# A two-layer decoder on one core: transposed copies of x made by VectorE and DMAs instead of TensorE, in cross attention and in local attention

## The reference

```python
x = _layernorm(x + _L0_attn_ref(x, ...))            # state space model
x = _layernorm(x + _L0_xattn_ref(x, ctx, ctx, mask, ...))   # cross attention
x = _layernorm(x + _L0_ffn_ref(x, ...))             # three linears, tanh
x = _layernorm(x + _L1_attn_ref(x, ...))            # local attention
x = _layernorm(x + _L1_xattn_ref(x, ctx, ...))
x = _layernorm(x + _L1_ffn_ref(x, ...))

def _L0_xattn_ref(q, k, v, mask, ...):
    qh = (q @ Wq.T + bq) ...                         # 16 heads of 32
    ...
    scores = jnp.where(mask, einsum('bhqd,bhkd->bhqk', qh, kh) / sqrt(D_K), -1e9)
    out = einsum('bhqk,bhkd->bhqd', softmax(scores), vh) ...
    return out @ Wo.T + bo

def _L0_ffn_ref(x, weight, aux_weight1, aux_weight2, bias):
    ...
    return jnp.tanh(x @ weight @ aux_weight1 @ aux_weight2 + bias)

def _L1_attn_ref(x, Wg, bg, Wv, bv, Wo, bo):
    g = x @ Wg.T + bg
    v = x @ Wv.T + bv
    ...
```

## Time and profile before

| | us |
|---|---|
| median of 3 runs | 2664.42 (2663.80 to 2665.64) |
| the profiled execution's own time | 2665.74 |
| its span in the trace | 2664.0 |
| TensorE busy | 2535.6 (95%) |
| VectorE busy | 1933.4 (73%) |
| GpSimd busy | 867.0 (33%) |
| ScalarE busy | 732.0 (27%) |

### The profile page before, as it was taken

One profiled execution on the slowest core, in us unless ns is written; L12 is line 12 of the kernel. 1 busy time (PEld: TensorE's weight loads), 2 busy tenths in 40 slices (PEclk: granted clock), 3 DMA queues, 4 the chain that ended last, 5 costly groups with the idle time before them and its releaser, 6 DMA issues. The chain is left out here.

```text
span 2664.0 us, 37090 instructions
## 1 busy us (share of the span) xinstructions
PE 2535.6 (95%) x12933; PEld 1562.9 (59%) x12933; DVE 1933.4 (73%) x3292; ACT 732.0 (27%) x1073; POOL 867.0 (33%) x900
## 2 busy tenths in 40 slices
PE   8999998999999898999998869999999999999998
PEld 4444544555555444445444447777777777777775
DVE  4788403666667446777778858888888888888886
ACT  1111222333332125666668711000000000000000
POOL 2322203455555336767677721111111111111000
PEclk9999999999999999999999989999999999999999
DMA  5444121000000043343434441222222222222111
GB/s 177 146 143 178 56 91 42 1 0 1 1 1 1 23 103 96 101 106 97 104 102 129 134 122 42 53 53 53 53 54 54 54 54 54 54 54 54 46 38 38
DMA packets 338726, 183.85 MB, mean 69 GB/s; under 512 B 174031, under 2 KB 304463, under 8 KB 337518
## 3 DMA queue, kind: packets, MB, share of 16 engines
q1 hardware_dynamic: 307862, 156.49, 21.4%
q10 hardware_dynamic: 30680, 24.98, 3.3%
HBM read 90.51 MB, written 52.43 MB: 54 GB/s over the span
## 5 line engine op out<-in xcount | busy, mean ns | idle before, releaser
L2114 PE MATMUL bank<-tiles,tl_XQT 128*128 128x512 f32 (+1 forms) x768 | 323.9, 565 | 1.2 <-issue 1.2
L2119 PE MATMUL bank<-tiles,tl_XQT 128*128 128x512 f32 (+1 forms) x768 | 317.9, 557 | 0.0
L2131 PE MATMUL bank<-tiles,tl_HT 128*128 128x512 f32 x682 | 302.1, 599 | 5.8 <-DMA tl_HT<-tl_tmp 5.8
L2114 PEld LDWEIGHTS bank<-tiles,tl_XQT 128*128 128x128 f32 x768 | 235.6, 309 | 79.8 <-issue 16.0
L2119 PEld LDWEIGHTS bank<-tiles,tl_XQT 128*128 128x128 f32 x768 | 236.7, 308 | 65.6
L2193 ACT ACTIVATE tl_HQ<-bank 128x512 f32<-128x512 f32 (+1 forms) x96 | 54.0, 562 | 803.1 <-PE bank L2114 757.0
L2131 PEld LDWEIGHTS bank<-tiles,tl_HT 128*128 128x128 f32 x682 | 219.3, 324 | 74.4 <-issue 9.4
L1403 POOL TENSOR_SCALAR_AFFINE_SELECT tiles<-tiles 128x512 f32<-128x512 f32 x256 | 184.0, 721 | 169.2 <-ACT tiles L1630 153.8
L2061 POOL TENSOR_TENSOR tl_rs<-tl_ve,mhalf 128x1 f32<-128x1 f32 x29 | 16.0, 551 | 527.5 <-DVE tl_ve L2272 527.5
L1730 DVE SCALAR_TENSOR_TENSOR tiles<-tiles,bank 128x1024 f32<-128x1024 f32 (+1 forms) x128 | 141.7, 1148 | 18.8 <-PE bank L1506 18.7
L1408 POOL TENSOR_SCALAR_AFFINE_SELECT tiles<-tiles 128x512 f32<-128x512 f32 x224 | 152.9, 682 | 0.0
(11 more groups left out here) (302 smaller groups left out, 4669.3 us busy)
## 6 DMA issues: line engine op xcount, KB each, us to landing
tl_HT<-tl_tmp SPq DMA_DIRECT2D x248, 44.0 KB, 2.0
tl_HT<-tl_tmp ACTq DMA_DIRECT2D x248, 44.0 KB, 2.0
fp_weights<-space_quant ACTq DMA_DIRECT2D x33, 256.0 KB, 2.1
X<-in_x SPq DMA_DIRECT2D x8, 1024.0 KB, 10.2
v<-tiles SPq DMA_DIRECT2D x32, 256.0 KB, 2.4
unit_g<-tiles SPq DMA_DIRECT2D x32, 256.0 KB, 2.5
unit_gT<-tiles SPq DMA_DIRECT2D x128, 64.0 KB, 2.1
la_GN<-unit_g SPq DMA_DIRECT2D x128, 64.0 KB, 2.1
```

The lines of the kernel that those rows point to most:

```text
L2114: mm = e.matmul(bank[(2 * q) % 3][:, 0:w], chunk(XQT[n % 2], c), WgT[q][:, :, c, :], start=(c == 0), stop=(c == C - 1))
L2119: mm = e.matmul(bank[(2 * q + 1) % 3][:, 0:w], chunk(XQT[n % 2], c), WuT[q][:, :, c, :], start=(c == 0), stop=(c == C - 1))
L2131: mm = e.matmul(bank[DOWN][:, :], chunk(HT, q), WdT[:, q, :], start=(q == 0), stop=(q == IC - 1))
```

## The change

In cross attention, tiles 0 to 7 are still transposed by TensorE. For tiles 8 to 31 VectorE transposes the 32x32 blocks into `XB` (`x_turned`), and SyncE moves them with 16 DMAs per tile into `XT` (`x_moved`). For x2 of tiles 0 to 29 VectorE writes the transposed blocks to `XB2` in another order (`x2_turned`), SyncE stores them to DRAM with 4 DMAs (`x2_stored`), and ScalarE's queue loads the tile back with one DMA; the last two still go through TensorE. `linear` moves back by one slot and stands ahead of `weigh`, and the two banks change turns accordingly. `added` and its `normal` come one slot later, ahead of `biased`. In local attention, tiles 2 to 31 go by VectorE, a store of 4 DMAs and a load of one, both on SyncE. Its buffer `XB` is shared with `AE`, which is used at the end of that stage.

```diff
@@ cross_attention_and_linears
+        BY_PE = 2 * B
+        later = lambda n: BY_PE <= n < NT
+        SLOTS = range(-2 * B, NT + 6)
+        by_blocks = lambda n: 0 <= n < NT - 2
...
             @block.sync
+                def x_moved(n):
+                    g, at = n // B, n % B * P
+                    e.wait_ge(s_xt.sem, s_xt.at(n - BY_PE + 1))
+                    e.wait_ge(s_q.sem, s_q.at(C * (g - 1)))
+                    for i in range(4):
+                        for j in range(4):
+                            e.dma_start(XT[g % 2][32 * j:32 * j + 32, :, at + 32 * i:at + 32 * i + 32],
+                                        XB[n % 2][32 * i:32 * i + 32, :].rearrange("p (c j t) -> p j c t", c=C, j=4)[:, j]
+                                        ).then_inc(d_xt[n % 2].sem, 16)
+                def x2_stored(n):
+                    e.wait_ge(s_tu.sem, s_tu.at(n + 1))
+                    e.wait_ge(d_xl.sem, d_xl.at(16 * (n - 1)))
+                    for i in range(4):
+                        e.dma_start(k.X2d[n % 2].rearrange("(j p) w -> p j w", j=4)[:, :, P * i:P * i + P],
+                                    XB2[n % 2][32 * i:32 * i + 32, :].rearrange("p (j w) -> p j w", j=4)).then_inc(d_tu[n % 2].sem, 16)
...
+                for s in SLOTS:
+                    if by_blocks(s - 3):
+                        x2_stored(s - 3)
+                    if later(s + 2 * B):
+                        x_moved(s + 2 * B)
...
             @block.tensor
                 def query(i):
-                    e.wait_ge(s_tc.sem, s_tc.at(B * g + B))
+                    e.wait_ge(s_tc.sem, s_tc.at(min(B * g + B, BY_PE)))
+                    for d in d_xt:
+                        e.wait_ge(d.sem, d.at(256 * (B // 2) * (g - 1)))
...
+                def linear(n):
+                    s = n + 4
+                    if by_blocks(n):
+                        e.wait_ge(d_xl.sem, d_xl.at(16 * (n + 1)))
...
                 for s in SLOTS:
-                    if there(s + 2 * B):
+                    if 0 <= s + 2 * B < BY_PE:
                         transpose_x(s + 2 * B)
...
                         query(s + B)
+                    if there(s - 4):
+                        linear(s - 4)
                     if there(s - 2):
                         weigh(s - 2)
-                    if there(s - 3):
+                    if there(s - 3) and not by_blocks(s - 3):
                         transpose_x2(s - 3)
...
-                    if there(s - 3):
-                        linear(s - 3)
...
             @block.scalar
+                    if by_blocks(s - 3):
                         n = s - 3
+                        e.wait_ge(d_tu[n % 2].sem, d_tu[n % 2].at(64 * (n // 2 + 1)))
                         e.wait_ge(s_l.sem, s_l.at(n))
+                        e.dma_start(XLT, k.X2d[n % 2]).then_inc(d_xl.sem, 16)
...
             @block.vector
+                    if later(s + 2 * B + 1):
+                        x_turned(s + 2 * B + 1)
                     if there(s):
                         shifted(s)
                     if there(s - 2):
                         attended(s - 2)
                         normal(s - 2, mv2, rs2, s_r2, s_x2)
+                    if by_blocks(s - 2):
+                        x2_turned(s - 2)
@@ local_attention
+        BY_PE = 2
+        by_blocks = lambda m: BY_PE <= m < NT
...
             @block.sync
                     if part == 0:
+                        if by_blocks(m + 2):
+                            n = m + 2
+                            e.wait_ge(s_xd.sem, s_xd.at(n - BY_PE + 1))
...
+                            for i in range(4):
+                                e.dma_start(k.X1d[n % 2]..., XB...).then_inc(d_xs.sem, 16)
...
+                        if by_blocks(m + 1):
+                            n = m + 1
+                            e.wait_ge(d_xs.sem, d_xs.at(64 * (n - BY_PE + 1)))
+                            e.wait_ge(s_v.sem, s_v.at(n - 1))
+                            e.dma_start(XT[n % 2], k.X1d[n % 2]).then_inc(d_xt[n % 2].sem, 16)
...
             @block.vector
+                    if part == 1 and by_blocks(m + 3):
+                        x_turned(m + 3)
```

More of the change, by code:

```diff
@@ L79, in __init__ @@
         self.GTd, self.AOd = self.dram("unit_gT", (B * C, P, T)), self.dram("attended", (P, B * C, T))
+        self.X2d = self.dram("x2_turned", (2, P, D))
+        self.X1d = self.dram("x_turned", (2, P, D))
         self.YD = self.dram("half_log_norm", (B, 3 * H, T), BF16)
@@ L873, in cross_attention_and_linears @@
         XT, QT = w.XT, w.QT
+        XB = [sb(f"XB{n}", [P, D]) for n in range(2)]
+        s_xt, d_xt = sem("x_turned"), [sem(f"xT_moved{n}") for n in range(2)]
         RS = 3
@@ L885, in cross_attention_and_linears @@
         turn = lambda n, i: 5 + (3 * n + i) % 2
+        BY_PE = 2 * B
         x_bank = lambda n: n if n < B else XTB
+        later = lambda n: BY_PE <= n < NT
         x_tile = lambda n: k.x_tile(n % B, n // B)
         there = lambda n: 0 <= n < NT
-        SLOTS = range(-2 * B, NT + 5)
+        SLOTS = range(-2 * B, NT + 6)
+        by_blocks = lambda n: 0 <= n < NT - 2
+        XB2 = [sb(f"XB2{n}", [P, D]) for n in range(2)]
+        XLT = XL[:, :, :].rearrange("p c t -> p (c t)")
+        in_chunks = lambda x: x.rearrange("p (t c) -> p c t", c=C)
+        s_tu, d_tu, d_xl = sem("x2_turned"), [sem(f"x2_stored{n}") for n in range(2)], sem("x2T_load")
         with k.nc.Block() as block:
@@ L1137, in added, with x_turned, x2_turned @@
                     statistics(n, y, st3, mv3, ve3, s_a3, s_t3, s_m3, s_v3, s_r3)
+                def x_turned(n):
+                    e.wait_ge(d_xt[n % 2].sem, d_xt[n % 2].at(256 * ((n - BY_PE) // 2)))
+                    e.transpose(XB[n % 2][:, :], x_tile(n)).then_inc(s_xt.sem, 1)
+                def x2_turned(n):
+                    e.wait_ge(s_x2.sem, s_x2.at(n + 1))
+                    e.wait_ge(d_tu[n % 2].sem, d_tu[n % 2].at(64 * (n // 2)))
+                    e.transpose(XB2[n % 2][:, :].rearrange("p (j r c) -> p c j r", j=4, r=32), x_tile(n)).then_inc(s_tu.sem, 1)
                 e.wait_ge(s_bq.sem, s_bq.at(16))
@@ L1142, in _ @@
                 for s in SLOTS:
+                    if there(s - 1):
+                        total(s - 1)
+                    if there(s - 5):
+                        added(s - 5)
                     if there(s - 4):
                         biased(s - 4)
-                    if there(s - 1):
-                        total(s - 1)
-                    if there(s - 4):
-                        added(s - 4)
                     if there(s):
                         masked(s)
-                    if there(s - 4):
-                        normal(s - 4, mv3, rs3, s_r3, s_x3)
+                    if there(s - 5):
+                        normal(s - 5, mv3, rs3, s_r3, s_x3)
+                    if later(s + 2 * B + 1):
+                        x_turned(s + 2 * B + 1)
                     if there(s):
@@ L1182, in local_attention @@
         piece = lambda n, w=1: k.tiles[:, DOWN_AT + n * D:DOWN_AT + (n + w) * D]
-        XT = [piece(n).rearrange("p (c t) -> p c t", c=C) for n in range(2)]
+        XT = [piece(n) for n in range(2)]
+        in_chunks = lambda x: x.rearrange("p (t c) -> p c t", c=C)
+        BY_PE = 2
+        by_blocks = lambda m: BY_PE <= m < NT
+        XB = sb("XB", [P, D])
+        s_xd, d_xs, d_xt = sem("x_turned"), sem("x_stored"), [sem(f"xT_load{n}") for n in range(2)]
         Gs, SG, GH, VS, GQ = ([piece(n + i) for i in range(m)] for n, m in ((2, 2), (4, 1), (5, 2), (7, 2), (9, 2)))
@@ L1711, in _ @@
                     if part == 0:
-                        if tile(m + 1):
+                        if 0 <= m + 1 < BY_PE:
                             x_transposed(m + 1)
@@ L1820, in unit_turned, with x_turned @@
                     e.transpose(GQ[m % 2], GH[m % 2]).then_inc(s_gc.sem, 1)
+                def x_turned(m):
+                    e.wait_ge(d_xs.sem, d_xs.at(64 * (m - BY_PE)))
+                    e.transpose(XB[:, :].rearrange("p (j r c) -> p c j r", j=4, r=32), tile_x(m)).then_inc(s_xd.sem, 1)
                 def y_parts(b):
```

84 lines of the change are left out of this document (45 added, 39 removed).

## The result

The changed kernel takes 2699.89 us (median of 4 runs, 2697.95 to 2701.68), the kernel before, run beside it, 2665.03 (2663.80 to 2668.03). The ratio is 1.0131, with a 95% interval from 1.0119 to 1.0144: slower by about 35 us. The forecast was slower by 16.6. The profiled execution of the changed kernel has a span of 2700.0 us, against 2664.0.

The account below looks back on a forecast made before the run. TensorE was taken as the bound before, VectorE at 14.2 us per slot after, with SyncE's queue deciding. Cross attention +28.6 and local attention -12.0 give +16.6: 2665.7 + 16.6 - 1.3 = 2681 us, range 2652 to 2700 (own range 2664 to 2692).

Parts of the forecast that it names:

- The wait behind SyncE's queue: Cross attention: the query waits 5.9 us in slots 4, 8, ... 24 for moves queued behind x2's stores.
- The clock per wait: Cross attention: each query wait also costs 2.0 us through a slower TensorE clock, bounds 0 and 2.9.
- VectorE as the bound of a full slot, at 14.2: Cross attention: VectorE needs 14.2 us per slot, TensorE 14.02, so 0.75 of 0.93 us is left to gain.
- The moved linear ... Cost nothing: Cross attention: linear, now ahead of the scores, adds no cost; its non-adjacent weight loads hide behind matmuls of 0.43 us.
- a second wait of linear: Cross attention: sign that the prediction is wrong, if linear is seen waiting behind its load.
- A gain of 0.38 per tile, 21 tiles: -8.0: Later local attention: without transposes dots waits only for `biased`, gaining 0.38 us per tile, -8.0 us over 21 tiles.
- Local attention's first part: Start of local attention: a tile takes 6.86 us instead of 7.30, -4.0 us over nine tiles.
- the 6.1 us under 6.86: First part of local attention: stores, issues and load take 6.1 us, fitting under the tile's 6.86.
- in time: Rival, cross attention: 16 moves issued in under 3.7 us, no query wait, 2635 us; chance 0.17.
- in part: Rival, cross attention: at 0.45 us per issue the query waits 2.9 us, clock mostly kept, 2662 us; chance 0.12.
- That rival's 2698: Rival, cross attention: clock also falls between waits, 3 us lost in each of slots 28 to 31, about 2698; chance 0.05.
- The whole duration of a transpose: Rival, both stages: each tile gives back 1.09 us, not 0.44 to 0.49; 2628 us; chance 0.02.

Follow-up runs that it names:

- the kernel with the moves first and banks of their own: Changed kernel with SyncE's 16 x moves ahead of the x2 stores, plus fixed separate banks for linear and project from slot 28: 2648.34 us, ratio 0.9927.
- the kernel with the moves first: Changed kernel with one edit: in SyncE's queue the 16 moves of an x tile stand ahead of the 4 x2 stores: 2649.72 us, ratio 0.9944.
- the kernel with x2's late tiles by TensorE: Changed kernel with x moves ahead of x2 stores, and x2 of tiles 24 to 31 transposed by TensorE again: 2651.89 us, ratio 0.9956.

## Why the forecast was off

The sign and the first mechanism were right, the size was not: +35 against +16.6, outside the forecast's own range of 2664 to 2692 and at the edge of the wide one, 2652 to 2700. Two steps failed, each a term that was held to be safe: that the moved linear costs nothing, and that each tile of local attention's rounds gives back 0.38 us.

**The wait behind SyncE's queue: right.** Worked out 5.9 us in slots 4, 8, ... 24, measured 5.66 to 5.69 in five and 8.37 in the first. From `masked` to the query 24.0 us forecast (18.1 + 5.9), 24.06 measured (503.35 to 527.41). The wait vanishes when the order is turned, and follows the count of moves behind the stores.

**The clock per wait: 2.0 taken, 2.5 to 2.7 measured.** I took a value below the upper bound of 2.9 and said so; a wait of 5.7 us is longer than the 2.27 and 0.94 us of the earlier trace rows and lies nearer to the bound. From the query to the next `masked` it is 12.68 us for 11.9 (527.41 to 540.09), of which linear's exposed weight load is 0.1; the two slots ahead take 28.25 and not 28.4. A group costs 64.9 for 64.3, which is 3.0 us for the five, and the five took 298.6 before and not 299.0: 3.4 together.

**VectorE as the bound of a full slot, at 14.2: the other way round, at little cost.** A full slot takes 14.12 us with TensorE busy without a gap (14.02 and the 0.1 of the weight load), and VectorE's own work is 13.98, as the slots without a query show.

**"The moved linear ... Cost nothing": this step failed.** I had asked what it waits for in a full slot, where the query covers it, and carried the answer over to slots 28 to 35, where there is no query. There it waits for the bank that project had, until VectorE has added that product: 15.3 us in six times, twice followed by a slowed product (849.11 and 906.66, 5.49 us each, with a granted clock of 0.61 to 0.76). The prediction named a second wait of linear as a sign that it was wrong, but for its load. By the slots of the forecast: from `masked` of slot 24 to that of slot 27 I had -0.9 and it is -1.2 (42.37 for 43.55); from there to slot 31 +4.1 and it is +4.8 (57.55 for 52.71), since VectorE's own work is 13.98 and not 14.2 in a slot, but the slowed product adds 1.6; from slot 31 to the end -2 and it is +3.0 (43.42 for 40.39). In the kernel with the moves first and banks of their own, the end takes 40.20 us and no late linear is slowed. So I estimate the bank at 4.8 of the 5.7 us missed here (1.6 + 3.2); the rest is mostly the gain of 2 at the end, which did not come.

**"A gain of 0.38 per tile, 21 tiles: -8.0": this step failed too.** The rounds gained nothing. The one half of the error is that I let dots follow `biased` in 0.06 us, while it takes 0.21. The other is the weight load: I had called loads from columns that are not adjacent hidden in cross attention, and did not ask in local attention, where the product follows a matmul of another shape. A removed 0.54 us gave 0.11, and the round between gave back 0.12. Local attention's first part came out at -4.0 as forecast, and partly by luck. In the trace with local attention alone five of the nine tiles give back 0.44 us, the first takes 0.15 more, and the next two after the five give 0.25 together: there a G product waits 0.28 us for its load, which the 6.1 us under 6.86 had ruled out. The last gives 1.77 (9.71 for 11.48), since TensorE waits 0.81 and not 2.19 us for VectorE ahead of the transposes of `la_Y`. In the kernel before:

```profile
979.17 1.05 PE L1577 MATMUL bank<-ident,la_Y 128*48 128x128 f32 x8 [2.19 <-DVE la_Y L1838]
```

With local attention alone changed:

```profile
973.51 1.06 PE L1602 MATMUL bank<-ident,la_Y 128*48 128x128 f32 x8 [0.81 <-DVE la_Y L1866]
```

The rest of the -5.2 I cannot place. Together -5.2 and not -12.

So 40.6 - 5.2 = 35.4 stands against 28.6 - 12.0 = 16.6. Of the 18.8 us between them 6.8 are local attention, and 12.0 cross attention: in its trace 5.7 from slot 24 to the end, 3.4 in the groups, 0.9 at the start, and 2.0 more that its own run shows beyond the changed kernel's trace. Of these, 1.6 are in the trace with cross attention alone: there a third late product of linear is slowed, and slot 31 takes 15.56 us for 13.98. Why the clock fell in one execution and not in the other, stays open.

```profile
895.67 5.49 PE L1068 MATMUL bank<-space_T,space_quant 128*128 128x512 f32 x8 [2.93 <-issue]
```

**Rivals.** The moves were not in time, nor in part: 16 of them took 10.24 us, 0.64 each. The clock fell, but behind the waits and in single late slots. That rival's 2698 lies 2 us from the measured time, and this is luck: it had 12 us lost in slots 28 to 31, where the trace shows 1.6, and local attention's -12, of which 5.2 came. The whole duration of a transpose did not count: in the kernel with the moves first the slot on TensorE went from 14.95 to 14.12 us, 0.83 for two groups of transposes. The Trainium skill ("TensorE: Matmul & The Clock Gate", Part 4) gives 275 ns for one transpose in a kernel's context. That each of several in a row counts whole was my reading and not the page's; by this estimate the eight would have meant 2.2 us, and the trace does not bear it out.

## What to carry over

When an instruction moves, list its waits once for every phase of the loop, the run-out too: what covered a wait in full slots may be gone there. A gain is the distance to the second-latest wait, measured with its own latency and with the new durations of what feeds it, not the length of what was removed. And when a queue gets new work, the order of the new items among themselves can decide the sign: here two lines that changed places were worth 50 us.

## What was not expected of the hardware

- The clock's loss is not in proportion to the wait. From the query's start to linear's start: 3.44 us with no wait, 3.51 behind waits of 0.53 and 1.68 us, 5.21 behind 2.07 and 3.10, 6.38 behind 4.50, 5.96 to 6.10 behind 5.66 to 5.69, and 6.23 behind 8.37.
- Waits of the same length do not always cost the clock. In the kernel with x2's late tiles by TensorE linear waited 2.83 us in five slots on end and took 5.26, 5.49, 3.79, 3.79 and 5.49 us. Why, stays open.
- A DMA's issue costs SyncE by its form: 16 moves between places in SBUF 10.24 us, four stores to DRAM 1.76 (2.06 in pieces of 128 bytes), a load of the whole tile 0.38.
- A weight load of 128x128 float32 with columns 16 bytes apart takes 309 ns, 190 with adjacent ones.
- The same program's time varies by 3 us or more between executions (the kernel before: 2662.4 to 2667.8 in 16 runs), so that one trace showed local attention's gain as nothing. The 11 executions with that stage alone show it. Even where the code is the same the stage varies: 652.1 us in the kernel before and 655.1 in the trace with cross attention alone.
